# Attention of one Trainium2 kernel rewritten: hyperbolic heads in units of four heads by 32 queries, exponentials of two heads in one instruction, cosine keys normalised beforehand

## What is computed

```
qkv = x @ qkv_w.T ; q, k = rotary(q), rotary(k)        # 16 heads, 16 channels each
heads 0..5   (dot):        softmax(q k^T / sqrt(16) + causal) v
heads 6..9   (hyperbolic): tq = sqrt(1/c + sum q^2), tk = sqrt(1/c + sum k^2)
                           arg = max(-c (q k^T - tq tk^T), 1 + 1e-7)
                           softmax(1 / (1e-6 + sqrt(1/c) arccosh(arg)) + causal) v
heads 10..15 (cosine):     q, k divided by their norms; softmax(sqrt(16) q k^T + causal) v
x = layernorm(x + attention @ proj_w.T + proj_b)
x = layernorm(x + experts(x) + bias)
```

## Time and profile before

| | |
|---|---|
| median of 3 runs | 2585.75 us (2576.32 to 2589.16) |
| profiled execution, its own time | 2584.16 us |
| its span (first to last instruction) | 2582.6 us |
| busy PE, PEld | 1959.1 us (76%), 1028.0 us (40%) |
| busy DVE, ACT, POOL | 1592.2 us (62%), 1629.3 us (63%), 329.0 us (13%) |
| mean granted TensorE clock | 0.863 of full speed |

### The profile page before, as it was taken

One profiled execution on the slowest core, in us unless ns is written; L12 is line 12 of the kernel. 1 busy time (PEld: TensorE's weight loads), 2 busy tenths in 40 slices (PEclk: granted clock), 3 DMA queues, 4 the chain that ended last, 5 costly groups with the idle time before them and its releaser, 6 DMA issues. The chain is left out here.

```text
span 2582.6 us, 40426 instructions
## 1 busy us (share of the span) xinstructions
PE 1959.1 (76%) x12338; PEld 1028.0 (40%) x12338; DVE 1592.2 (62%) x3515; ACT 1629.3 (63%) x2414; POOL 329.0 (13%) x196
## 2 busy tenths in 40 slices
PE   6888898357687778877877787787787778766883
PEld 3344344123333343333334333333333333335773
DVE  4676667547657667766766777676677667661002
ACT  1333333248987977896797789679679978931110
POOL 0000000001211211121121111112112122210002
PEclk9999999668788878988887898888789888887997
DMA  4233222550340341143035023303502420027773
GB/s 177 104 112 142 99 99 99 141 87 1 67 84 2 60 95 31 18 76 93 1 67 108 12 35 76 76 1 67 118 2 36 99 69 16 14 70 267 277 261 122
DMA packets 90824, 218.08 MB, mean 84 GB/s; under 512 B 16689, under 2 KB 37042, under 8 KB 86258
## 3 DMA queue, kind: packets, MB, share of 16 engines
q1 hardware_dynamic: 82162, 185.01, 27.3%
q0 software_dynamic: 8448, 30.41, 3.7%
HBM read 146.59 MB, written 68.78 MB: 83 GB/s over the span
## 5 line engine op out<-in xcount | busy, mean ns | idle before, releaser
L1086 POOL TENSOR_TENSOR a_R<-a_Z 128x258 f32<-128x258 f32 (+7 forms) x128 | 270.3, 2111 | 1857.5 <-DVE a_Z L1162 1678.9
L845 PE MATMUL a_s<-a_Q,a_K 96*128 96x512 bf16 (+7 forms) x1152 | 420.1, 374 | 72.9 <-DMA a_K<-qk_parts 23.3
L874 PE MATMUL a_w<-a_K,a_Q 96*128 96x512 bf16 (+5 forms) x960 | 329.8, 364 | 126.6 <-DVE a_mx L1170 52.3
L1017 ACT ACTIVATE a_PT<-a_s,a_rk 128x512 f32<-128x512 f32 (+3 forms) x576 | 327.9, 579 | 147.6 <-PE a_s L848 98.1
L885 PE MATMUL a_w<-a_ident,a_R 128*128 128x128 f32 x1152 | 234.7, 332 | 183.0 <-ACT a_R L1046 181.9
L1017 ACT ACTIVATE a_PT<-a_s 128x512 f32<-128x512 f32 (+3 forms) x576 | 276.0, 491 | 107.7 <-PE a_s L848 97.1
L1170 DVE TENSOR_REDUCE a_mx<-a_w 128x1 f32<-128x512 f32 (+2 forms) x576 | 307.4, 550 | 42.6 <-PE a_w L877 22.5
L1162 DVE TENSOR_SCALAR_CACHE_REDUCE a_Z<-a_w 128x512 f32<-128x512 f32 (+3 forms) x384 | 210.3, 554 | 191.2 <-PE a_w L877 111.5
L860 PE MATMUL a_o<-a_PT,a_V 128*32 128x512 f32 (+3 forms) x2304 | 298.9, 597 | 0.1
L885 PEld LDWEIGHTS a_w<-a_ident,a_R 128*128 128x128 f32 x1152 | 153.3, 168 | 310.4 <-issue 175.4
L254 PE MATMUL p_ps<-p_xT,p_w 128*128 128x512 f32 x512 | 247.4, 639 | 36.0 <-DVE p_fac L484 20.1
(11 more groups left out here) (161 smaller groups left out, 2689.4 us busy)
## 6 DMA issues: line engine op xcount, KB each, us to landing
e_w<-in_w SPq DMA_DIRECT2D x23, 2048.0 KB, 7.8
qk_parts<-p_parts SPq DMA_DIRECT2D x32, 768.0 KB, 3.5
a_Q<-qk_parts SPq DMA_DIRECT2D x144, 128.0 KB, 4.1
a_K<-qk_parts SPq DMA_DIRECT2D x144, 128.0 KB, 6.1
v_rows<-p_vt SPq DMA_DIRECT2D x8, 2048.0 KB, 7.7
a_V<-v_rows SPq DMA_DIRECT2D x32, 512.0 KB, 7.0
p_xin<-in_x SPq DMA_DIRECT2D x8, 1024.0 KB, 6.8
a_X<-in_x POOLq DMA_DIRECT2D x8, 1024.0 KB, 8.7
```

The source lines that it names most:

```text
L845: m = pe.matmul(bank[:, 0:w], Kb[0:r, h, P * j:P * j + P], Qb[0:r, h, t0:t0 + w], start=True, stop=not diag)
L874: m = pe.matmul(bank[:, 0:w], Qb[0:r, h, P * i:P * i + P], Kb[0:r, h, s0:s0 + w], start=True, stop=not diag)
L1017: act.activation(PT[:, u % 2, k, 0:w], sB[x % 3][:, 0:w], ACT.Exp, scale=scale).then_inc(prob.sem, 1)
L1086: pool.tensor_tensor(R[:, n % RB, :, 0:ww], Z[:, n % 2, :, 0:ww], Z[:, n % 2, :, 0:ww], ALU.mult) \
```

## The change

In `project`, `rk`, `columns` and the DMA to `rk_cols` go. The clamp, the two ScalarE functions and the multiplication that served group 0 (queries) serve group 3 too, which holds the cosine keys: `clamp_norms(b, 1)` behind `cut(2)`, `scale(b, 1)` behind the copies of the values, ahead of `cut(3)`. TensorE gets the norms' product once more.

In `attend`:
- PSUM: `sB` is two buffers of two banks. TensorE writes the scores of two heads, then one ScalarE instruction takes the exponential of both with a constant scale. There are 72 of these in a turn in place of 144.
- The hyperbolic work is in 8 units. A unit has all four heads on the 128 partitions, 32 queries each, and takes two groups of 64 queries, one late and one early (groups 15 and 0, 14 and 1, ...), in two halves each: 2176 elements in each partition for every unit, and 6 columns for minima. An argument's bank is filled by four matmuls of 32 output columns, one for each head (48 banks in a turn, as before).
- Each chain step is one instruction for a unit: `log_square`, `root`, `log_sum`, `log_distance`, `inverse`, each 8 times in a turn; `hyp_exp` is 32 instructions, without a tensor as scale. The curvature's factor is in the exponent's bias of `inverse`.
- The diagonal's mask is applied by GpSimd in `R` ahead of the transposes; VectorE copies only. `hyp_values` goes through the ring of three banks, and the bank `oh` is gone.
- The table: a unit starts every 15 slots, with fixed distances. The root's addition stays on VectorE (it stood there before too).
- `X3` is gone: the bias is added in place, so VectorE waits until `x_mid` has been written. GpSimd's DMAs are items of the table.

```diff
@@ project @@
+                if not first:
+                    pe.wait_ge(ra_ready.sem, ra_ready.at(b - 1))
                 product(1, True, slot[0])
...
+                norms(0)
...
+                norms(3)
...
                 cut(2)
+                clamp_norms(b, 1)
...
+                scale(b, 1)
                 cut(3)
@@ attend: the table @@
+        NU, QH, GK = 8, 32, 64
+        UW = 17 * 2 * GK
+        def unit(n):
+            e, odd = divmod(n, 2)
+            return e, (NT * 2 - 1 - 2 * e - odd, 2 * e + odd)
-            work[2 * n + 1][0].append(("log_square", n))
-            work[2 * n + 1][2].append(("root", n))
-            work[2 * n + 1][3].append(("add_root", n))
...
+        PERIOD = 15
+        for n in range(NU):
+            ready = NSLOT + PERIOD * n
+            args = [("argument", n, k, pc) for k, seg in enumerate(segments(n)) for pc in range(len(seg[3]))]
+            span = 2 * len(args) if n else NSLOT
+            for a, item in enumerate(args):
+                put(ready - span + a * span // len(args), item)
+            put(ready, ("square", n))
+            put(ready + 4, ("log_square", n))
+            put(ready + 6, ("root", n))
+            put(ready + 7, ("add_root", n))
+            put(ready + 10, ("log_sum", n))
+            put(ready + 12, ("log_distance", n))
+            put(ready + 14, ("inverse", n))
+            put(ready + 16, ("row_bias", n))
+            for k in range(4):
+                put(ready + 18 + 2 * k, ("hyp_exp", n, k))
+            for part, at in ((0, 21), (1, 26)):
+                put(ready + at, ("mask", n, part))
+                for q in range(len(turns(n, part))):
+                    put(ready + at + 1 + part + q, ("turn", n, part, q))
+            if n % 2:
+                for part in range(2):
+                    put(ready + 33 + part, ("hyp_values", HYP_TILES[n - 1 + part]))
...
+        work[28][3].append(("mid_out",))
+        work[29][3].append(("add_bias",))
@@ attend: TensorE @@
+                for i in range(2):
+                    h = GROUPS[g][2 * k + i]
+                    m = pe.matmul(sB[x % 2][:, i, 0:w], Kb[0:r, h, P * j:P * j + P], Qb[0:r, h, t0:t0 + w],
+                                  start=True, stop=not diag)
...
+                for h in range(N_HYP):
+                    m = pe.matmul(bank[QH * h:QH * h + QH, 0:w], Qb[0:r, HYP0 + h, q0:q0 + QH],
+                                  Kb[0:r, HYP0 + h, s0:s0 + w], start=True, stop=not diag)
...
+                    pe.wait_ge(h_masked.sem, h_masked.at(b, 2 * n + part))
@@ attend: ScalarE, GpSimd, VectorE @@
-                act.activation(PT[:, u % 2, k, 0:w], sB[x % 3][:, 0:w], ACT.Exp, scale=scale).then_inc(prob.sem, 1)
+                act.activation(PT[:, u % 2, 2 * k:2 * k + 2, 0:w], sB[x % 2][:, :, 0:w], ACT.Exp,
+                               scale=scale_of(GROUPS[g][2 * k])).then_inc(prob.sem, 1)
...
+                    pool.tensor_tensor(edge, edge, hmasks[:, 1], ALU.mult).then_inc(h_masked.sem, 1)
...
-                    dve.wait_ge(normed.sem, normed.at(d, 0))
-                    dve.tensor_tensor(X3[:], X[:], bias2[:].unsqueeze(1).to_broadcast([P, NT, C]), ALU.add) \
+                    dve.wait_ge(mid_sent.sem, mid_sent.at(d))
+                    dve.tensor_tensor(X[:], X[:], bias2[:].unsqueeze(1).to_broadcast([P, NT, C]), ALU.add) \
                         .then_inc(biased.sem, 1)
```

More of the change, by code:

```diff
@@ L303, in turn @@
                 m.then_inc(rows_ready.sem, 1)
-            def columns(d):
-                hold(pe, r_step.sem, r_step.at(d, 3), pe_passed)
-                for n in range(NT):
-                    m = pe.transpose(slot[0][:, n * 16:(n + 1) * 16], rr[:, n * P:(n + 1) * P], ident[0:16, 0:16])
-                m.then_inc(cols_ready.sem, 1)
             turn(0, first=True)
@@ L689, in last_turn @@
         def last_turn(n):
-            return wide["turn", n, len(turns[n]) - 1]
+            return wide["turn", n, 1, len(turns(n, 1)) - 1]
         def r_before(n):
@@ L876, in row_scores @@
                 if diag:
-                    m = pe.matmul(bank[:, w - P:w], identb[:], masksb[:, mask, :], start=False, stop=True)
+                    m = pe.matmul(bank[:, w - P:w], identb[:], masksb[:, 1, :], start=False, stop=True)
                 m.then_inc(wide_full.sem, 1)
-            def turn_pair(b, n, q):
-                if q == 0:
-                    pe.wait_ge(h_prob.sem, h_prob.at(b, 2 * n + 1))
-                bank = wide_bank(b, wide["turn", n, q])
-                for a, (j, k) in enumerate(turns[n][q]):
-                    m = pe.transpose(bank[:, a * P:(a + 1) * P], R[:, n % RB, k, P * j:P * j + P], ident[:])
-                m.then_inc(wide_full.sem, 1)
@@ new lines, in turn_probs @@
+            def turn_probs(b, n, part, q):
+                if q == 0:
+                    pe.wait_ge(h_masked.sem, h_masked.at(b, 2 * n + part))
+                bank = wide_bank(b, wide["turn", n, part, q])
+                if turns(n, part)[q][0][1] < P:
+                    pe.sem_inc(pe_passed, 1)
+                for a, (j, w) in enumerate(turns(n, part)[q]):
+                    for half in range(2):
+                        at = segments(n)[2 * part + half][2] + P * j
+                        out = bank[0:w, a * 2 * P:(a + 1) * 2 * P].rearrange("p (h f q) -> p h f q", h=N_HYP, f=2)
+                        m = pe.transpose(out[:, :, half, :], R[:, n % RB, at:at + w], ident[:])
+                m.then_inc(wide_full.sem, 1)
@@ L896, in apply_hyp_values @@
+            def apply_hyp_values(b, tile):
+                e, part = (tile, 1) if tile < NT // 2 else (NT - 1 - tile, 0)
+                n = 2 * e + 1
+                pe.wait_ge(wide_free.sem, wide_free.at(b, wide["turn", n, part, len(turns(n, part)) - 1]))
+                bank = wide_bank(b, wide["hyp_values", tile])
+                if e == 0 and part == 0:
+                    pe.wait_ge(v_here[3].sem, v_here[3].at(b))
+                for j in range(tile + 1):
                     for k in range(4):
-                        m = pe.matmul(oH[VW * k:VW * k + VW, o:o + P], V[:, 3, j, k, :], PTh[:, j, k, :],
-                                      start=(j == 0), stop=(j == i))
@@ L899, in apply_hyp_values @@
[L899 to L900 removed]
+                        m = pe.matmul(bank[VW * k:VW * k + VW, 0:P], V[:, 3, j, k, :], PTh[:, home(n, part, j), k, :],
+                                      start=(j == 0), stop=(j == tile))
+                m.then_inc(wide_full.sem, 1)
             def turn_sums(b, d, n, x):
@@ new lines, in turn @@
+            def turn(b, is_first=False, is_last=False):
+                for u, step in enumerate(work):
+                    for slot in step:
+                        for item in slot:
+                            if item[0] == "mid_out" and not is_first:
+                                rows_out(b - 1, x_mid, 0, mid_sent)
+                            elif item[0] == "rows_out" and not is_first:
+                                rows_out(b - 1, io["out"], 1, out_sent)
+                            elif item[0] == "rows_in" and not is_first:
+                                hold(pool, out_sent.sem, out_sent.at(b - 1), pool_passed)
+                                rows_in(b)
+                            else:
+                                do(b, item)
+                    if is_last and u % 4 == 1 and u // 4 < NT:
+                        load_rows(u // 4)
+                    if is_last and u % 4 == 3 and u // 4 < NT:
+                        spread_rows(u // 4)
```

483 lines of the change are left out of this document (225 added, 258 removed).

## The result

The changed kernel takes 2622.84 us (median of 4 runs, 2618.42 to 2623.17), the kernel before 2581.03 us (4 runs): a ratio of 1.016, 95% interval 1.012 to 1.019. It is 1.6% slower, where 2465 us was forecast. The profiled execution took 2618.42 us, its span is 2616.8 us, 34.2 more than before.

A forecast was written before the change was run, and what follows sets the result against it. No engine was full in an attention turn; each lasts as long as the fullest engine and its waits. From 2584.16 us, -144 for eight turns, +15 projections, +10 at the end gave 2465 us; own range 2415 to 2520.

The forecast's parts named there:

- How it lies in time: Attention turn, split in two parts: 118 us and 86 us, so 204 us in place of 222, -144 us over eight turns.
- I take 13: First part of a turn: 13 us of waiting on top of TensorE's 105 us, giving 118 us; bounds 108 and 126.
- 75 + 7 = 82: Second part of a turn: TensorE's 75 us of work plus 7 us, most of its wait for exponentials gone.
- 4 for the bias: Second part of a turn: VectorE's bias waits about 4 us for `x_mid`, bounds 0 and 7; 10 us at the end.
- Four heads side by side: Argument matmuls on TensorE: four heads run side by side, next matmul some 0.35 us behind; 7 us more a turn.
- Rival 3: Argument matmuls: the four heads do not run side by side, 22 us longer a turn, 2641 us; 0.08 with other losses.
- Rival 2: First part of a turn: three engines near 90% in order, turn 218 us, time 2577, no change; 0.2 with rival 4.
- Rival 4: Root's addition on VectorE: the root comes late, waits 21 us a turn for 7.0, time 2577; 0.2 with rival 2.
- Rival 1: Attention turn: ScalarE alone decides, turn 190 us, time 2353 us; chance 0.17.
- Projections +15: Projections: second clamp, second multiplication and one more crossing, less what is given back, cost 15 us; bounds 0 and 29.
- The chances: Whole kernel: forecast 0.55; faster by more than half a per cent 0.87, within it 0.06, slower 0.07.
- What would show it: Profile after: wrong if TensorE does not limit the first part, or waits for exponentials stay at 24 us.

The follow-up runs named there:

- chain moved: Changed kernel with only the hyperbolic chain later in the table: root's addition and bias two slots, exponentials one, masks three, turnings two; 2494.99 us, ratio 0.967.
- the run with later turnings: Changed kernel with mask, turning and values of each hyperbolic unit four slots later in the table; 2656.96 us, ratio 1.029.
- four wide banks: Changed kernel with exponentials per head, three score buffers of one head and four wide banks for three; 2552.45 us, ratio 0.993.
- single score banks: Changed kernel with four score buffers of one head each and one exponential per head, three wide banks; 2603.74 us, ratio 1.011.
- the halves: Changed kernel with each root's addition as two instructions of half the columns, in slots 7 and 8 of a unit; 2577.91 us, ratio 1.003.
- four wide banks and 14 slots: Kernel with three single score banks and four wide banks, units 14 slots apart instead of 15; 2491.86 us, ratio 0.974.
- four wide banks as well: Kernel with three single score banks and four wide banks, with the hyperbolic chain moved later in the table too; 2433.29 us, ratio 0.948.

## Why the prediction was wrong

The step that failed is "How it lies in time": *a turn is 118 + 86 = 204 us*, and in it the terms for waiting, *I take 13* and *75 + 7 = 82*, with 4 for the bias. They are 24 us of standing TensorE in a turn; it was 45.1. TensorE's and ScalarE's work came out within 4 us in each part; VectorE's was 6 us over in the second (60.2 for 54).

- *ScalarE, VectorE, TensorE in a turn*: 153.9, 147.0 and 176.4 us, for 153, 143 and 180 (105 + 75). *Four heads side by side*: 0.33 us for 0.35. Rival 3 is out.
- *What waits in the first part, I take 13*: 22.6. *In the second, 75 + 7 = 82, and 4 for the bias*: 22.5. I had argued that two slots and four between `hyp_exp` and the turning, "where there was one", would take most of the 24.0 us away. They took half (12.3). The distance in slots has to be held against how far TensorE runs ahead of ScalarE, two pairs of heads, which is four slots, and against what stands on ScalarE between: steps of 2.0 to 2.1 us where the mean of L1027 was 1.2. The waits for wide banks, which the working did not price, rose from 18.9 to 21.6.
- *204 us and the moved chain*: moved by one to three slots, to four and five between `hyp_exp` and the turning, it brought the turn to 208.9. That this is near 204 is in part luck, since two errors offset each other. Over five turns TensorE still stood 39 us in each and not 24, but its work was 170 us and not 180, at the higher granted clock. The working took TensorE's work as independent of the waits.
- *Rival 2, "the first part eats it" (turn 218, no change)*, came nearest in numbers (123.7 + 97.8). But its reason, three engines too full in order, does not hold: chain moved has the same work in the same order of kinds and a turn of 208.9.
- *Rival 4, the root comes late*: 1.8 us in this turn, not 21, and yet it was part of the matter. It was hidden by the other stall, and the run with later turnings brought it out (14.8). I had counted the two as separate risks with prices that add.
- *Rival 1, ScalarE alone decides*: no. With four wide banks its work is 158 us in a turn at 214, 199 and 194 us.
- *The wide ring*: in the working three banks were a given and VectorE's 2.4 us additions had a price only for VectorE. While one runs, or is waited for, TensorE stands behind three full banks: 3.64 us at 1225.76. The fourth bank took 51 us off the kernel with single score banks, the halves 38 to 45 off the changed one.
- *The loop's jump*, not in the working at all: 6.5 us of TensorE's time in place of 3.7, as the input rows now load there (issued at 1415.33, 3.3 us ahead of the stop, before at 1395.31, 10.6 ahead).
- *The wait for `x_mid`, 4 us in a turn and 10 at the end*: none in this turn, 5.7 at the end. ScalarE and TensorE were late enough to hide it: in the faster kernels some of it shows (1.9 us in the turn with the chain moved, 3.9 with four wide banks and 14 slots).
- *Projections +15*: +14.5 to the first argument matmul; the further 3.1 to the first square are the first unit's own arguments.
- *The sum*: of the miss of 153 us in the profiled execution, 137 lie in the first seven turns (-126 forecast, +10.5 measured), 14 in the last with the end (-8, +6.1), and under 3 ahead of them.
- *The chances*: 0.07 for slower had only rival 3 and unnamed losses behind it; a stall that moves from one place to the next had no rival. By their own terms the chances of faster add up to 0.85, not 0.87. *What would show it* did not help either: TensorE was the fullest engine in the first part and the waits for exponentials did not stay at 24 us, so by these two signs the prediction looked right while the turn was 17 us longer than forecast.

## What to carry to other kernels

In a hand-written table in which engines run ahead of one another, count for each item that waits on another engine the slots between the two, and hold them against how far its engine can run ahead (buffers of scores, wide banks) plus the longest instruction that now stands between. When instructions are fused into fewer and longer ones this distance has to grow with them, and all items that wait for the same engine have to move together: one stall removed alone shows the next. Sum up every wait of the fullest engine before one of them is called the cause. Look at what loads while an engine jumps back in its loop.

## What the hardware showed that was not expected

- TensorE's busy time for the same 7011 records moves with the stalls. Over five turns of the loop it was busy 179 us a turn in the changed kernel at a mean granted clock of 0.81, 170 with the chain moved at 0.85, 164 with four wide banks as well at 0.88; it stood 44, 39 and 35 us in a turn. In the 10 us behind the jump at 1425 us, after 6.5 us in which it stood, the granted clock was 0.50, that is the lower of the two levels, 1.2 GHz:

```profile
1418.00:1425.00 7.00, 0.59 (x24) 0.32 (x12) 0.91 (x2) 0.00 (x0) 0.00 (x0) 0.80 0.84 231
1425.00:1435.00 10.00, 9.85 (x57) 4.41 (x58) 5.91 (x20) 2.05 (x2) 1.72 (x1) 0.50 0.91 196
```

  and a matmul of 512 columns took 0.60 us for 0.39. The Trainium skill (TensorE: Matmul & The Clock Gate, What's actually happening) has the throttled state as the default, which activity releases; these rows agree. In the 10 us from 1410 us of the kernel before, behind a stall of 3.7 us, the mean was 0.83. So a long stall seems to cost more than its own length, but no run changes the clock by itself, and the sum of the waits alone does not set it: with its other matmuls the kernel before stood 49 us in a turn at 0.86.
- At a loop's jump an engine can stand for 3.2 to 9.2 us with no semaphore to wait for, and what decides is whether a large load was issued some microseconds ahead: of the same 1 MB of rows, 1.2 us or less ahead gave 3.6 to 4.2 us, 2.8 to 5.2 us ahead 4.8 to 9.2.
- Two ScalarE instructions with no semaphore between them overlap by some 0.1 us (1.09 us for two of 512, 0.595 for one), so fusing them saved 0.07 us and not the 0.17 us of fixed time that one alone shows.
